# Key products before the exponential and sums, and fewer waits on PE, in a two-layer decoder's wide cross-attention

## The reference, cut to what matters

```python
xn = layernorm(x)                          # (128, 128) per batch element
q, k, v = xn @ w_q, ctx @ w_k, ctx @ w_v   # 16 heads of 64, 77 keys
p = softmax(q @ k.T * 64 ** -0.5)          # (16, 128, 77)
x = x + tanh(gate) * (p @ v @ w_out + b_out)
```

## Time and profile before

| | |
|---|---|
| median of 3 runs | 3024.32 us (3020.64 to 3024.77) |
| the profiled execution, its own time | 3028.85 us |
| its span in the profile | 3027.0 us |
| PE busy | 2734.3 us (90%) |
| DVE, ACT, POOL busy | 2098.6, 1911.7, 1944.2 us |
| mean granted TensorE clock | 0.958 |
| wide cross-attention (x_... tiles of L756 to L1158) | from about 460 to 1250 us |

### The profile page before, as it was taken

One profiled execution on the slowest core, in us unless ns is written; L12 is line 12 of the kernel. 1 busy time (PEld: TensorE's weight loads), 2 busy tenths in 40 slices (PEclk: granted clock), 3 DMA queues, 4 the chain that ended last, 5 costly groups with the idle time before them and its releaser, 6 DMA issues. The chain is left out here.

```text
span 3027.0 us, 82766 instructions
## 1 busy us (share of the span) xinstructions
PE 2734.3 (90%) x27846; PEld 2311.3 (76%) x27847; DVE 2098.6 (69%) x4560; ACT 1911.7 (63%) x4300; POOL 1944.2 (64%) x3245
## 2 busy tenths in 40 slices
PE   7999987999999999499997999995899999999996
PEld 6788766888888888388885888873677777777775
DVE  4777655677666666345555999997777878878543
ACT  3666544666666666255553777774778777777762
POOL 4566534556666666426667999985677777867652
PEclk9999998999999999699997999995899999999998
DMA  8566530000000000222222000000000000000000
GB/s 234 179 190 190 168 104 20 2 10 14 12 12 14 11 14 14 74 69 82 82 82 56 1 0 0 0 0 1 2 2 8 5 9 5 5 8 5 8 5 11
DMA packets 204792, 129.08 MB, mean 43 GB/s; under 512 B 13840, under 2 KB 197112, under 8 KB 203896
## 3 DMA queue, kind: packets, MB, share of 16 engines
q1 hardware_dynamic: 196344, 108.80, 12.1%
q0 software_dynamic: 8192, 16.79, 1.9%
HBM read 35.05 MB, written 90.51 MB: 41 GB/s over the span
## 5 line engine op out<-in xcount | busy, mean ns | idle before, releaser
L1558 PE MATMUL a_ps_s<-a_qk,w_ident 128*128 128x256 f32 x1024 | 239.1, 387 | 19.5 <-POOL a_qk L1665 18.4
L1013 POOL TENSOR_TENSOR x_p<-x_p,x_rz 128x1232 f32<-128x1232 f32 x64 | 143.9, 2248 | 170.0 <-DVE x_rz L1122 169.0
L635 DVE TENSOR_REDUCE a_nmax<-a_ps_s 128x4 f32<-128x512 f32 x256 | 164.9, 686 | 113.5 <-PE a_ps_s L381 109.9
L1665 POOL TENSOR_TENSOR a_qk<-a_qkv 128x2048 f32<-128x2048 f32 x64 | 235.5, 3680 | 2.6 <-POOL a_eight L218 1.0
L479 ACT ACTIVATE a_e<-a_ps_s 128x512 f32<-128x512 f32 x256 | 138.9, 595 | 151.2 <-PE a_ps_s L386 151.2
L1558 PEld LDWEIGHTS a_ps_s<-a_qk,w_ident 128*128 128x128 f32 x1024 | 192.3, 193 | 49.9 <-POOL a_qk L1665 22.1
L2384 POOL TENSOR_TENSOR x_sq<-x_e 128x1232 f32<-128x1232 f32 x64 | 143.2, 2237 | 125.2 <-DVE x_t_sq L2543 125.0
L1639 ACT ACTIVATE a_r<-a_o,w_a_rows 128x128 f32<-128x128 f32 x512 | 220.6, 521 | 2.4 <-DVE a_o L1724 1.7
L1393 POOL DMA_INDIRECT f_yg<-f_rows_out,f_index x120 | 115.1, 959 | 154.3 <-DVE f_yo L1473 137.9
L895 ACT ACTIVATE x_uu_hi<-x_ps_u 128x308 fp32r<-128x308 f32 x256 | 101.9, 423 | 111.5 <-PE x_ps_u L758 111.2
L1129 DVE TENSOR_REDUCE x_top<-x_ps_s 128x16 f32<-128x1232 f32 x64 | 91.2, 1424 | 114.4 <-PE x_ps_s L758 114.4
(11 more groups left out here) (627 smaller groups left out, 9648.2 us busy)
## 6 DMA issues: line engine op xcount, KB each, us to landing
f_rows_in<-a_zeros SPq DMA_DIRECT2D x31, 1088.0 KB, 5.4
f_rows_out<-a_zeros SPq DMA_DIRECT2D x31, 1088.0 KB, 8.8
f_xin<-f_rows_in SPq DMA_DIRECT2D x135, 64.0 KB
f_rows_out<-f_yo SPq DMA_DIRECT2D x135, 64.0 KB, 1.6
out<-x SPq DMA_DIRECT2D x16, 256.0 KB, 2.3
f_raw<-in_late_f SPq DMA_DIRECT2D x2, 1408.0 KB, 6.3
w_ctx<-in_ctx SPq DMA_DIRECT2D x1, 2464.0 KB
f_rows_in<-f_xr,f_where POOLq DMA_INDIRECT x128, 2.3
```

Source lines behind the costliest of these rows:

```text
L635: nc.vector.tensor_reduce(nmax[:, u % 2, g, :], ps_s[g][:, :].rearrange("p (t k) -> p t k", t=GROUP), AX.X, ALU.max, negate=True).then_inc ...
L1013: nc.gpsimd.tensor_tensor(wide, wide, rz[:, :].unsqueeze(2).broadcast_to([P, HEADS, K]), ALU.mult).then_inc(p_ready, 1)
L1558: ins = nc.tensor.matmul(ps_s[u % 2][:, 0:HEADS * HEADS], c.ident[:, :], qk[:, u % 2, k, :, :], start=k == 0, stop=k == HD - 1)
L1665: nc.gpsimd.tensor_tensor(qk[:, u % 2, :, :, :], qkv[:, u % UNROLL, 0, :, :].unsqueeze(3).broadcast_to(full), qkv[:, u % UNROLL, 1, :, :]. ...
```

## The change

1. DVE: the subtractions of key products 2 and 3 move from behind the statistics to right behind "scores minus maximum", ahead of xr, the addition and the statistics. The sum z and reciprocal rz move from the head of the next slot to the end of the slot that scores the element, behind xn and ahead of `rank` and `place`.
2. ACT: the copies of key products 2 and 3 move ahead of the exponential.
3. PE: in the loop, waits are left out where another wait or PE's own order implies them; the slots written out keep them all. A loop body has 480 rows before and 413 now.

POOL's code and SP's are unchanged.

```diff
 def scores(at):                                    # PE
     pe.wait_ge(x_lo_ready, s + 1)
-    wait(pe, d_ready, s)
-    pe.wait_ge(u_ready, 4 * (s - u % 4 + 4))
+    if sl_fixed(at):
+        wait(pe, d_ready, s)
+    if sl_fixed(at) or u % 4 == 0:
+        pe.wait_ge(u_ready, 4 * (s - u % 4 + 4))
     for g in range(GROUPS):
-        wait(pe, pT_ready, 4 * (s + SCORE - WEIGH - 1) + g + 1)
+        if sl_fixed(at):
+            wait(pe, pT_ready, 4 * (s + SCORE - WEIGH - 1) + g + 1)
+        elif g % 2 == 0:
+            pe.wait_ge(pT_ready, 4 * (s + SCORE - WEIGH - 1) + g + 2)
...
 def projected(at, some):                           # PE
-    pe.wait_ge(keys_lo_ready, s - u % 4 + 4)
+    if sl_fixed(at) or u % 4 == 0 and some[0] == 0:
+        pe.wait_ge(keys_lo_ready, s - u % 4 + 4)
...
 def outputs(at, half):                             # PE
-    if half == 0:
+    if half == 0 and sl_fixed(at):
         pe.wait_ge(pT_ready, (s + 1) * 4)
         pe.wait_ge(v_ready, 2 * (s + 1))
...
 def values(at, half):                              # PE
-    pe.wait_ge(cx_lo_ready, s + 1)
+    if half == 0:
+        pe.wait_ge(cx_lo_ready, s + 1)
...
-    wait(pe, v_ready, 2 * (s - 1) + half + 1)
+    if sl_fixed(at):
+        wait(pe, v_ready, 2 * (s - 1) + half + 1)
...
 def slot(sl):                                      # ACT
     if valued:
         outputs(valued, 0)
+    if at := sl.step(0):
+        projected(at, (2, 3))
     if at := sl.step(SCORE):
         nc.scalar.activation(p, p, ACT.Exp, ...)
-    if at := sl.step(0):
-        projected(at, (2, 3))
...
 def slot(sl):                                      # DVE
-    if at := sl.step(WEIGH):
-        z = sum of p; rz = reciprocal of z
     if at := sl.step(SCORE):
         ...
         nc.vector.tensor_tensor(p, data, each, ALU.subtract).then_inc(d_ready, 1)
+    if at := sl.step(0):
+        projected(at, (2, 3))
     if at := sl.step(ROUTE):
...
         nc.vector.bn_stats(c.stats[:, s, :], c.x[:, s, :]).then_inc(stats_done, 1)
-    if at := sl.step(0):
-        projected(at, (2, 3))
     if at := sl.step(NORM):
...
+    if at := sl.step(SCORE):
+        z = sum of p; rz = reciprocal of z
     if (at := sl.step(RANK)) and at[1] % BATCHES == 0:
```

More of the change, by code:

```diff
@@ L813, in transposes @@
                         pe.wait_ge(d_ready, min(scored, B) if sl_fixed(at) else scored)
-                    wait(pe, pT_ready, 4 * (s - 1) + g + 1)
+                    if sl_fixed(at):
+                        wait(pe, pT_ready, 4 * (s - 1) + g + 1)
                     for j in range(GROUP):
@@ L844, in slot @@
                     wait(pe, r_ready, s + LAST - ROUTE)
-                    pe.wait_ge(oT_ready, 2 * (s + 1))
+                    if sl.fixed:
+                        pe.wait_ge(oT_ready, 2 * (s + 1))
                     turned = s + LAST - TURN
                     wait(pe, xT_ready, min(turned, B) if sl.fixed else turned)
-                    wait(pe, x_done, s)
+                    if sl.fixed:
+                        wait(pe, x_done, s)
                     for n in range(PAIRS):
@@ L863, in slot @@
                     pe.wait_ge(xn_ready, s + 1)
-                    wait(pe, xT_ready, s)
+                    if sl.fixed:
+                        wait(pe, xT_ready, s)
                     wait(pe, x_done, s + TURN - LAST + 1)
@@ L869, in slot @@
                     pe.wait_ge(xr_ready, s + 1)
-                    wait(pe, rT_ready, s)
-                    wait(pe, r_ready, s)
-                    wait(pe, x_done, min(s + ROUTE - LAST + 1, B) if sl.fixed else s + ROUTE - LAST + 1)
+                    if sl.fixed:
+                        wait(pe, rT_ready, s)
+                        wait(pe, r_ready, s)
+                        wait(pe, x_done, min(s + ROUTE - LAST + 1, B))
                     nc.tensor.transpose(ps_rT, xr[:, u, :], c.ident[:, :]).then_inc(rT_ps, 1)
@@ L875, in slot @@
                     s, u = at
-                    ranked = s + PLACE - ROUTE
-                    pe.wait_ge(r_ready, min(ranked, B) if sl.fixed else ranked)
+                    if sl.fixed:
+                        pe.wait_ge(r_ready, min(s + PLACE - ROUTE, B))
                     pe.wait_ge(mask_ready, s + BATCHES)
@@ L1159, in slot @@
                                             ALU.subtract, ALU.mult).then_inc(xn_ready, 1)
+                if at := sl.step(SCORE):
+                    s, u = at
+                    dve.wait_ge(exp_done, s + 1)
+                    wait(dve, p_ready, s)
+                    nc.vector.tensor_reduce(z[:, :], p[:, u % 2, :, :, :].rearrange("p g j k -> p (g j) k"), AX.X,
+                                            ALU.add).then_inc(z_done, 1)
+                    dve.wait_ge(z_done, s + 1)
+                    nc.vector.reciprocal(rz[:, :], z[:, :]).then_inc(rz_done, 1)
                 if (at := sl.step(RANK)) and at[1] % BATCHES == 0:
```

## The result

The change made the kernel **slower**: 3048.26 us median of 8 runs (3038.54 to 3054.85) against 3027.68 us of the kernel before on the same chip (8 runs, 3020.64 to 3034.27); ratio 1.0066, 95% interval [1.0046, 1.0086]. Forecast were 3023.0 us and a range up to 3032.

A forecast was written before the change was run, and what follows sets the result against it. PE was taken to bound the wide cross-attention, only slots over the floor having recoverable waits. Gain -16.8 plus price 15.4 gave -1.4 us, from the 3024.32 median to 3023.0 us; range 3007 to 3032.

The forecast's parts named there:

- The gain, -16.8: Slots 1 and 5 fall to the floor, 10.9 us; before the loop 5.3; last slots 0.6.
- Statistics 1.9 us later, GpSimd's chain shifted whole: VectorE's late statistics delay GpSimd's chain by 1.9 us; PE pays 0.4 in slots 3 and 7, 1.4 in slot 4.
- At slot 0 the hole at the branch covers it.: In slot 0 the later keys_lo costs PE nothing, hidden in its 1.76 us idle after the backward branch.
- the equal slots: Slots before the loop (11.07 us, constants) match loop slots (11.05, 11.06, registers): PE's sequencer costs the array nothing.
- I take 0: About 20 PE waits per slot left out gain 0; upper bound 21 us in 40 slots.
- Rank, now behind z, ... is hidden under PE's wait for keys_lo there.: In slot 4, rank ends later and pushes the maximum, hidden under PE's keys_lo wait; no cost.
- Half clock falls differently each time ... 1 to 2 us either way: Clock drops vary the whole time by 1 to 2 us either way; no term in the sum.
- Rival C: Five more clock drops, of 1.7 us each, at slots 4, before the loop and the branch: +7.1, 3031.4; chance 0.12.
- The exponential: On ScalarE it starts 1.6 us later, behind the copies; costs nothing, with 0.3 us of cover.
- rival D: ScalarE's transpose copies 0.5 us later than reckoned; some 56 slots lengthen by 0.2: +9.8, 3034.1; chance 0.07.
- Rival A: Gain alone: GpSimd's chain absorbs the delay or statistics are less late, keys_lo costs nothing more: -16.8, 3007.5; chance 0.16.
- Rival B: Pauses before PE's weight loads are the waits' and close: a further 21 us, 3002; chance 0.04.
- the two early chains: GpSimd's chain ends twice more without branch cover, at counters 20 and 24: 1.8 us each, 3.6 together.

The follow-up runs named there:

- the order alone: Changed kernel with all of PE's old waits put back, keeping the new order on VectorE and ScalarE: ratio 1.0084 to the kernel before.
- the 112 added waits a pass: Kernel before with the changed kernel's PE waits, plus 112 never-holding loop waits (46 more instructions per pass): ratio 0.9981 to the kernel before.
- the kernel with the keys early: Changed kernel with GpSimd making the keys of batches beginning in slot 4 two slots earlier, ahead of its statistics wait: ratio 1.0019 to the kernel before.
- the kernel with the ranks early: Changed kernel with VectorE's rank put back ahead of the sum and the reciprocal: ratio 1.0024 to the kernel before.
- the both-early kernel: Changed kernel with VectorE's subtractions back behind the statistics and rank back ahead of sum and reciprocal: 3026.78 us against 3050.23, ratio 0.9919.
- the statistics early: Changed kernel with VectorE's xr, output add and statistics back ahead of the subtractions of key products 2 and 3: ratio 0.9965 to the kernel before.

## Why the prediction was wrong, step by step

- **The gain, -16.8.** Right in place and size: slots 1 and 5 gave 12.9, the filling 4.0, together 16.9.
- **Statistics 1.9 us later, GpSimd's chain shifted whole.** Right: 1.84, from the bias add to the product. Slots 3 and 7 were forecast at 0.4 more each, ten times 0.4; measured +0.45 and, beside the branch's gain, +0.35: 2.3 in slots 3, and 1.8 in slots 7 (6.5 gained where the kernels without the wait gain 8.3). The keys' wait was forecast at 1.4 on top of 0.26, measured 1.77.
- **"At slot 0 the hole at the branch covers it."** The first step that failed. The hole was a consequence of the size of PE's loop body, which the change cut by 81 instructions. With it went the cover, in four slots 0: 5.1 us at full clock (four times 13.4, less 48.5 before). Where the hole stayed, in the kernel with the order alone, slot 7 grew by 1.4 to 2.0 us in place of the 0.4 and 0.2 of the sum, so the cover was not free there either. Since the equal slots 574.89 to 585.96 and 11.05 us showed only that waits cost nothing as they pass, not what their number does at the branch, **"I take 0" for the PE waits left out** failed with it: alone they gain 8.9 us by the ratio of 0.9971, 4.9 by the stage; in slots 7 of the changed kernel the branch gives 8.3, more than the lost cover costs at full clock. The 1.76 us of the earlier trace rows and "slot 0 follows the backward branch" stood in the prediction; that this hole might be removable was not asked. By the figure of the Trainium skill (Advanced Engine Details and Errata, Network/Comms) for reading a semaphore the prediction had an estimated 40 to 80 us for the waits, were they on the path; the 112 added waits a pass, 14 a slot, which moved no slot by more than 0.1 us, speak against such a price on the path.
- **"Rank, now behind z, ... is hidden under PE's wait for keys_lo there."** True in the loop of the changed kernel only, and not elsewhere: the slots behind the first and the last ranks have no such wait and grew by 3.5 and 3.6 us, part of it the clock. Slot 4 of the kernel with the keys early shows 0.8 us of it under the other wait. Undoing the statistics alone left it in slots 0 and 4, at 19.3 us of the stage.
- **"Half clock falls differently each time ... 1 to 2 us either way", and nothing for it in the sum.** This is the largest term that failed, and the one that took the time out of the range. Seven of nine waits of 1.8 us were followed by 1.2 GHz, at 3.15 us in four slots and about 1.6 in three: 17.4 us. PE stood at 1.2 GHz for 34 us more than before. Without these 17.4 us the slots would have grown by about 1.3 us, not 18.7. Rival C (+8.5, chance 0.12) had it right in kind, too small and too unlikely: it counted a drop at 1.7 us from one 4 us window, and the slots show up to twice that. How many waits are followed by a fall is not fixed: in the kernel with the ranks early it was four of nine. Matmuls back to back, as the Trainium skill (Perfetto Trace Analysis, Matmul Optimizations) wants them, agree with this: with both late things gone no stretch at 1.2 GHz began between the first and the last slot start.
- **The exponential, and rival D.** "Cost nothing" was right: floor slots stayed at 11.05 to 11.06. D did not happen.
- **Rival A** fell in this kernel; the both-early kernel is its case, and goes further than it. **Rival B** fell too: the pauses before the weight loads of the output products stayed (6.1 us in 34 cases, 6.4 in 35 before), though 166 waits a pass were gone.

Slots 0 and 4 account for the error: forecast +11.4 together with the two early chains and the branch, measured +39.8: 12.7 for the waits of nine loop slots at full clock (nine times 13.4, less 107.9 before), 17.4 for the clock in them, 9.7 for the three such slots ahead of those nine and the one behind them.

The last term, 9.7, is the ranks and the keys together, partly the clock; 3.6 were forecast for the two slots 4 and 0 ahead of the nine. Against the forecast of -1.4 the slots came out 20.1 us too long: 17.4 the clock, 5.1 the cover, 6 more ahead of and behind the nine, less 8.3 from the branch.

Open: why one 1.8 us wait is followed by half clock and the next, alike in the rows shown, is not. No run held the clock fixed, so its share is read from the slots and from the records of the clock.

## What to carry to other kernels

- An operation moved later is not priced by who waits for it but by everything that stands in the waiter's queue behind it: 1.84 us on VectorE came out in GpSimd's keys two slots later as 1.92. Moving that last piece ahead of the wait is an alternative to moving the cause.
- A hole that a step relies on as cover needs its own cause looked up in the changed program, not only in the old trace: here the same diff removed it. At a backward branch compare the branch's record, the instruction queue's packets and the number of instructions in the body.
- In a change of several moves some win and some lose, and the sum hides both: -16.9 and -6.5 against +39.8 here; undoing the two losing moves gave a kernel 0.8% faster than the one before.

## What the runs showed of the hardware

- TensorE's loop body was read anew at eleven of twelve backward branches at 780 and 785 instructions of the program (nine packets of 16 KB and 3.7 to 5.0 us each) and at none at 745 and 699 (0.2 us). The twelfth, at 780, took 0.23 us without a packet.
- A VectorE multiply of 128x32 that ran beside GpSimd's product (about 2.3 us) took 2.06 to 2.49 us and ended 0.04 to 0.06 us after the product, in all 13 cases of the twelve traces (ten of them with the statistics early); the 371 that met no product took 0.19 to 0.73.
- Waits of TensorE of 1.7 to 1.8 us within a busy stretch were followed by 1.2 GHz in seven of nine cases in the changed kernel and in four of nine with the ranks early; waits of 1.1 us with the statistics early were not followed by it in the loop.
